# One-hot tiles of two edge passes made by ScalarE as a square and a Relu, instead of a compare on VectorE

## What is computed

```python
# layer 0: messages relu(x[dst] @ Wa + x[src] @ Wb + edge_attr @ We + ...)
agg = jax.ops.segment_sum(msg, dst, num_segments=x.shape[0])
...
# layers 1 and 2, by h = x @ W + b, with batch norm behind each
msg = h[src] + edge_attr_emb_src
agg = jax.ops.segment_sum(msg, dst, num_segments=n_nodes) + h
return jax.nn.relu(agg) + bias
```

## Time and profile before

| | |
|---|---|
| median of 3 runs | 15650.02 us (15645.94 to 15651.08) |
| profiled execution, its own time | 15667.31 us |
| profiled execution, span of the core | 15665.6 us |
| mean granted TensorE clock | 0.559 |
| busy: TensorE matmul / VectorE / ScalarE / GpSimd | 44% / 32% / 3% / 60% |
| DMA | 688.51 MB, mean 44 GB/s |

### The profile page before, as it was taken

The page is one execution under the profiler, slowest core; times in us unless marked ns, Lnnn a source line. Parts: engine busy times, 40 slices in busy tenths (PEclk is TensorE's granted clock), DMA queues, the critical chain, the costliest instruction groups (busy, mean ns, idle before and its releaser), DMA issues.

```text
span 15665.6 us, 128029 instructions
## 1 busy us (share of the span) xinstructions
PE 6858.2 (44%) x29865; PEld 5870.1 (37%) x29865; DVE 4970.4 (32%) x12980; ACT 396.2 (3%) x790; POOL 9376.9 (60%) x9927
## 2 busy tenths in 40 slices
PE   3555665666666565333333333334333333333333
PEld 3455555555555555222222222223222222222222
DVE  1333333333333333233233323233332233233223
ACT  0000000000000000000000000000000000000000
POOL 5555555555555554666666666665666666666664
PEclk9666666556565655555555555555555555555555
DMA  2233333333333332111111212112111111111111
GB/s 57 65 67 67 68 68 67 67 68 68 67 69 67 67 69 47 34 34 34 34 34 34 34 34 35 34 34 46 24 23 23 23 23 23 23 23 23 23 23 33
DMA packets 1678916, 688.51 MB, mean 44 GB/s; under 512 B 1375841, under 2 KB 1518977, under 8 KB 1678734
## 3 DMA queue, kind: packets, MB, share of 16 engines
q1 hardware_dynamic: 1363181, 359.16, 11.0%
q0 software_dynamic: 315680, 328.70, 10.9%
HBM read 658.74 MB, written 28.14 MB: 44 GB/s over the span
## 4 chain that ended last, share of the span: by engine, by line
another core or an unknown queue 47%; DVE 18%; DVEq 14%; issue 11%; PE 8%; POOL 1%; DMA 0%; SPq 0%; ACT 0%; ACTq 0%; POOLq 0%
DVE by_rank L940 13%; DVEq L909 11%; PE sum_ps L653 4%; DVE hit L925 3%; PE pre_ps L630 1%; PE pre_ps L627 1%; DVEq L933 1%; DVEq L930 1%; DVEq L925 1%; DVEq L931 1%; POOL ranked L528 1%; DVE summed_in L919 1%; DVE scratch L913 0%; DVEq L335 0%
## 5 line engine op out<-in xcount | busy, mean ns | idle before, releaser
L546 POOL DMA_INDIRECT rows<-source_table,index x6250 | 5927.0, 948 | 4120.7 <-issue 2000.2
L940 DVE TENSOR_TENSOR by_rank<-by_rank,sum_ps 64x128 f32 (+1 forms) x9375 | 2626.0, 280 | 7858.2 <-remote 6978.5
L653 PE MATMUL sum_ps<-hit,message 128*64 128x128 f32 (+1 forms) x12500 | 2844.0, 404 | 3493.7 <-DVE hit L925 1462.8
L546 POOL DMA_INDIRECT message<-source_table,index x3125 | 2955.6, 946 | 1639.9 <-issue 888.1
L653 PEld LDWEIGHTS sum_ps<-hit,message 128*64 128x64 f32 (+1 forms) x12500 | 2375.0, 237 | 3845.3 <-issue 3780.9
L653 PE MATMUL sum_ps<-hit,rows 128*64 128x128 f32 x6250 | 1428.3, 412 | 3091.1 <-DVE hit L925 2056.6
L653 PEld LDWEIGHTS sum_ps<-hit,rows 128*64 128x64 f32 x6250 | 1205.0, 218 | 3314.1 <-issue 3307.4
L925 DVE TENSOR_TENSOR hit<-out_ps,edge_place 128x640 f32<-128x640 f32 x1875 | 1539.6, 821 | 1349.2 <-issue 1201.9
L627 PE MATMUL pre_ps<-w_edge,scratch 96*128 96x192 f32 x2500 | 983.0, 487 | 1356.3 <-DVE summed_in L919 867.9
L630 PE MATMUL pre_ps<-scratch 128*128 128x64 f32 x6250 | 1331.5, 360 | 462.0 <-issue 461.8
L630 PEld LDWEIGHTS pre_ps<-scratch 128*128 128x128 f32 x6250 | 1298.6, 280 | 538.9 <-issue 511.5
(11 more groups left out here) (156 smaller groups left out, 1413.5 us busy)
## 6 DMA issues: line engine op xcount, KB each, us to landing
rows<-source_table,index POOLq DMA_INDIRECT x6250
scratch<-ranked SPq DMA_DIRECT2D x3125, 32.0 KB
scratch<-place_rows SPq DMA_DIRECT2D x625, 160.0 KB
scratch<-in_edge_t_steps SPq DMA_DIRECT2D x625, 96.0 KB
message<-in_edge_steps SPq DMA_DIRECT2D x625, 80.0 KB
message<-source_table,index POOLq DMA_INDIRECT x3125
xt<-in_x_t SPq DMA_DIRECT2D x28, 224.0 KB
index<-in_src_steps SPq DMA_DIRECT2D x375, 12.5 KB
```

The costliest lines, as they stand in the source:

```text
L546: nc.gpsimd.indirect_dma_start(to, None, source_table[l][:, :], bass.IndirectOffsetOnAxis(ap=index[:, at.j, s:s + 1], axis=0))\
L653: one = mm(tile_sum(at.half, s)[0:w, :], (message if l < 2 else rows)[:, at.slot, s, 0:w], hit[:, at.half, s, :], start=True, stop=True)
L940: V.tensor_tensor(at_rank[s], at_rank[s], tile_sum(at.half, s)[0:w, :], ALU.add)\
```

## The change

In passes 1 and 2 the one-hots are made on ScalarE. For each tile of the step it takes Square(place − lane), which is 0 where the two agree and at least 1 elsewhere, then one Relu(1 − that) over all five tiles, which gives exactly 1 or 0. VectorE keeps the register loads and the additions. Pass 0 is untouched. ScalarE reads `along` in SBUF and not the copy in PSUM.

```diff
+        apart_made = [sem(f"apart_made{l}") for l in range(3)]
...
+                    m = at + 1
+                    if l and m.real:
+                        wait(act, tile_summed[l], m.number - 1)
+                        apart = [edge_place[:, bass.ds(m.number * S + s, 1)] for s in range(S)]
+                        for of in apart:
+                            act.lower_ap(of)
+                        for s in range(S):
+                            one = nc.scalar.activation(hit[:, m.half, s, :], along[:, :], ACT.Square,
+                                                       bias=apart[s], scale=-1.0)
+                        one.then_inc(apart_made[l], 1)
+                        act.wait_ge(apart_made[l], m.number + 1)
+                        nc.scalar.activation(hit[:, m.half, :, :], hit[:, m.half, :, :], ACT.Relu,
+                                             bias=1.0, scale=-1.0).then_inc(hit_made[l], 1)
...
-                pipeline(act, steps)
+                pipeline(act, steps, lead=1 if l else 0)
...
-                    if m.real:
+                    if l == 0 and m.real:
                         wait(dve, tile_summed[l], m.number - 1)
                         V.tensor_tensor(hit[:, m.half, :, :], over(along_ps, [P, S, P], 1),
```

## The result

The change is slightly slower. The kernel before took 15643.74 us (median of 9 runs, 15608.53 to 15651.08), the changed one 15680.65 us (9 runs, 15659.89 to 15694.71): a ratio of 1.0028, 95% interval 1.0018 to 1.0038. The profiled execution of it took 15678.76 us, with a span of 15677.0.

A forecast was written before the change was run, and what follows sets the result against it. Gathers plus GpSimd's wait for TensorE's stuck signals bound passes 1 and 2. Gains of 131 + 63 = 194 us, taken as 170, turn 15,667.3 into 15,497; the run median stands 17 lower: 15,480, range 15,250 to 15,800.

The forecast's parts named there:

- The bound: Passes 1 and 2: gathers are the floor, 6.25 us a step; only GpSimd's wait above it can be won, at most 1,230 us.
- The cost of the new instructions: ScalarE, passes 1 and 2: square 378 ns, five squares 1.5 us, Relu 0.74 us, whole chain 2.55 us a step.
- The estimate of 3.2 us: ScalarE's chain per step by the Trainium skill page's budget, about 0.3 us per activation plus 0.83 ns per element; set aside.
- When the sums come: After T, when stuck signals come out, sums start at T + 2.8, 5.4 and 8.0, previously T + 3.6, 7.1 and 10.6.
- Rival 2: Half of it: ScalarE's chain nearer 3.1 us, only a third of the gain comes, 15,590 us; chance 0.10.
- rival 3: Slower: chain above about 3.4 us, all bursts four steps, 15,790; if activations also add to the queue, 15,890; chance 0.22.
- The edge lies at about T + 9.5: Second sums ending before about T + 9.5 (T: stuck signals come out) are answered at once; moving to T + 7.8 allows five-step bursts.
- The long burst: Pass 2, five steps in 35.8 us, second sum answered at once; the short one, four steps, had its second addition 5.5 us late.
- messages of TensorE and SyncE queue up: Passes 1 and 2: unbroken gathers make signals stick until GpSimd stops about 4.4 us; SyncE index load 1.39 us against 0.39.
- Bursts of five and six steps: Passes 1 and 2: five-step bursts become the rule, some of six, 7.08 us a step against 7.29 and 7.18.
- Rival 1: Nothing changes within 30 us: gathers alone set burst length, signals after some 8 us are stuck; 15,650 us; chance 0.14.
- The prediction's last test: Passes 1 and 2: pauses coming closer although sums are earlier would say ScalarE's work itself holds up TensorE's signals.

The follow-up runs named there:

- kernel 2: The changed kernel, ScalarE starting a step's hits only after VectorE added the step two before; 12690.23 us, ratio 0.9999 to the kernel before, on a chip without pauses.
- kernel 1: The kernel before plus the six ScalarE activations per step into a spare buffer, VectorE keeping its compare; 12691.07 us against 12690.71, ratio 0.9999, no pauses.
- kernels 2 and 3: The second of these: the changed kernel with one 128x640 activation replacing six, one-hots not computed; 12692.32 us, ratio 1.0001 to the kernel before, no pauses.

## Why the prediction was wrong

Its range, 15,250 to 15,800, holds the time; its sign and its middle, 15,480, do not.

- **The bound.** Right. Five gathers of 1.25 us are the floor, which the executions without pauses run at, and what is above it in passes 1 and 2 is GpSimd's wait for late signals. "1,230 us at the very most" is right as well: of the 2,960 us between 15,650 and 12,690, these two passes account for the (7.29 − 6.25 + 7.18 − 6.25) x 625 = 1,230. The larger part, (8.8 − 6.29) x 625 = 1,570, is pass 0, whose waits were not followed here; the rest lies ahead of and between the passes.
- **The cost of the new instructions.** Right: 389 and 737 ns. Five squares took 1.57 us (1.5 forecast), and the chain from hit to hit 8012.33 − 8010.00 = 2.33 us (2.55). The estimate of 3.2 us was too long; the two rows of 470 and 577 ns that it was held against have no pointer bias in the kernel, while the budget is for one. The same page of the Trainium skill, "ScalarE: Activation LUTs", What ACT_TABLE_LOAD costs, has finer figures that I had passed over: 280 ns + 0.833 ns per element with a pointer bias, which is 387 ns at 128, and an overlap of some 93 ns between neighbours. The trace agrees: 389 ns, and (5 x 389 − 1570) / 4 = 94 ns.
- **When the sums come.** Right, within 0.3 us of the forecast in the burst shown. Rival 2 and rival 3 in its plain form fall with that: the chain is nowhere near 3.4 us.
- **"The edge lies at about T + 9.5, then, and moving the second sum to T + 7.8 puts it on the good side." This is the step that failed.** It took lateness for a matter of time since the restart. The second sum was moved to T + 7.7 and was later by 10.2 us in place of 5.5 in pass 1; in pass 2 it ended 6.6 us behind the restart, was stuck for 4.1 us, and before it had passed at 8.75. Over all bursts of pass 2 the median second sum came 1.7 us sooner and waited 6.2 us in place of 1.0. The two bursts from which the edge was read did not show one. The long burst has its T here:

```profile
11529.90 1.54 DVE L940 TENSOR_TENSOR by_rank<-by_rank,sum_ps 64x128 f32 x5 [11.22 <-remote]
```

So its second sum ended at 11539.36 − 11529.90 = T + 9.46 and was answered at once, while that of the short one ended at 8064.75 − 8055.23 = T + 9.52 and was stuck for 5.5 us. Moments 0.06 us apart had opposite fates; what differed was the pass (one was in pass 1, one in pass 2), and the time since T explained nothing. My reading now is that whatever fills up fills with what the engines do, and that the change makes it fill sooner by at least as much as it sends sooner. That is an inference, since nothing in the traces shows what fills up.

- **"While gathers run without a break, messages of TensorE and SyncE queue up."** Incomplete. The unbroken gathers of the other chips show no queue at all: answers within 0.03 us, and an index load of 0.39 us in SyncE in the middle of a run of gathers. The 1.39 us of the earlier trace rows is an extreme, and one such load stands in the trace without pauses too; but SyncE is slower in general. Of its index loads in passes 1 and 2 (rows above 0.1 us), 85 of 265 took over 0.5 us in the kernel before, and 4 of 248 in kernel 2 without pauses. The gathers may be needed for the lateness, but they are not enough for it; something in which these executions differ is needed too, and no view shows what.
- **Bursts of five and six steps.** Wrong: 29.1 us stayed the distance in pass 1, so its 131 us of gain were nothing, and pass 2, which was to go from 7.18 to 7.08 us a step for another 63 us, went to 7.26.
- **Rival 1** had pass 1 right, for the wrong reason (that any signal after some 8 us is stuck). **Rival 3's** clause "should the six activations of a step also add to what queues up" has the sign and is still alive; its price, +240 us, was far too large against the 37 and 73 us measured, since bursts of pass 2 went from five steps to four and hardly any from four to three. The prediction's last test, that ScalarE's work itself holds up the signals if the pauses come closer although the sums are earlier, came out as written in pass 2. The piling of paired sums would give the same reading, so I do not take it as shown.

That the change was worth something at all was right only on a condition: with two gathers a step it gains 235 us. At five, the chain behind a pause is not what bounds the kernel: shortening it left the pauses of pass 1 where they were and brought those of pass 2 closer.

What stays open is which half of the change makes the signals late. Kernels 1 and 2 would settle it on an execution with pauses; they met none.

## What to carry to other kernels

When a profile's own label is "remote" and the cure rests on when such a signal gets through, a threshold read from two bursts is a guess about a queue that nobody has seen. Tabulate all bursts first (here that would have shown second sums with the same end and 1.0 and 5.2 us of lateness), and price the change at nothing until an experiment that moves the signal has made it less late. Work taken off a chain is worth its time only where the chain sets the pace; here the same edit is 2.2% faster with two gathers a step, and 0.3 to 0.5% slower with five where signals are late; where they are not late, its variants (kernels 2 and 3) took the time of the kernel before. And measure a kernel of this kind on more than one chip before tuning it to its stalls: here the time differed by a fifth between them.

## What the runs showed of the hardware

The same program takes 12,680 to 12,690 us on some chips and 15,650 on others. The granted clock does not explain it: on average over the span it was 0.56 in both (0.561 and 0.559). What differs in passes 1 and 2 is how late TensorE's sums are answered: 0.03 us in kernel 2 without pauses, against a median of 8 us and up to 27 in the kernel before. Where the difference between the chips comes from, no run shows.

The traces differ too. That of the kernel before, with pauses, holds 68,265 records of semaphore updates, and that of kernel 1 on a chip without them 261,019. So in a trace with pauses the label of a wait ("remote", "issue") is less sure than its length.

Where sums came in pairs, TensorE's clock was higher. In pass 2 it was granted 0.57 in place of 0.52. The sum behind a pair, at 13462.55, took 1.28 us for ten matmuls at a granted clock of 1.00, where the same ten took 2.36 us at 0.50 in the sum of 11537.00: the levels of 2.4 and 1.2 GHz. TensorE had just worked 4.6 us almost without a gap. No time was gained by it; the engine is busy less than a third of the span of these passes.

The Trainium skill, "Perfetto Trace Analysis", Tensor Engine Instruction, says that a matmul's end in a profile is an estimate and that the semaphore update comes after it, once PSUM has acknowledged the writes. The runs without pauses put a bound on that, 0.03 us at 7006.07. So the 10 us from 8017.35 to 8027.54 are no error of the modelled end as it stands in those runs. The trace's own record of that update is stamped 8027.52, just ahead of the addition, so by this record it is the update that comes late, and not the engines that see it late. Whether the write to PSUM or the signal behind it takes the time, the profile does not show.
